# First tap of the scan's convolution made on GpSimd, and two units' first pieces projected a chunk sooner

## The reference

```python
zxbcdt = u @ Wi.T                        # z: 256, xBC: 512, dt: 4 columns
conv = jax.lax.conv_general_dilated(xBC_t, conv_w, (1,), 'VALID', feature_group_count=CONV_DIM, ...)
xBC = jax.nn.silu(jnp.moveaxis(conv, 1, 2) + conv_b)      # 4 taps along time, a filter for each channel
dt = jax.nn.softplus(dt + dt_bias)
def step(h, inp):                        # over the 1024 tokens
    dA = jnp.exp(dt_t * A)
    h = h * dA[..., None, None] + (dt_t[..., None] * x_t)[..., None] * B_t[:, None, None, :]
    y_t = jnp.einsum('bhpn,bn->bhp', h, C_t)
y = (y + D * x) * silu(z)
y = y * rsqrt(mean(y * y) + 1e-05) * norm_w
return y @ Wo.T
```

## Time and profile before

| | |
|---|---|
| median of 3 runs | 825.32 us (821.44 to 828.21) |
| the profiled execution, its own time | 819.01 us |
| its span, first to last instruction | 817.2 us |
| busy in the span: PE, DVE, ACT, POOL | 715.5, 489.4, 542.0, 275.2 us |
| mean granted TensorE clock | 0.955 of full speed |
| the scan's stretch, chunks 0 to 31 | about 471 to 674 us |

### The profile page before, as it was taken

How to read it: one execution, slowest core, us unless ns; L and a number is a source line. 1 busy time by engine, 2 the same in 40 slices (tenths; PEclk the granted TensorE clock), 3 DMA queues, 4 the chain that set the end, 5 groups by cost and what they waited for, 6 DMA issues and landing times. The chain is left out here.

```text
span 817.2 us, 13088 instructions
## 1 busy us (share of the span) xinstructions
PE 715.5 (88%) x4076; PEld 377.9 (46%) x4076; DVE 489.4 (60%) x1424; ACT 542.0 (66%) x934; POOL 275.2 (34%) x296
## 2 busy tenths in 40 slices
PE   4799999979999997988988867798888987999996
PEld 1432222212223223555655545576575775566564
DVE  6878442204766565763466649789697875533453
ACT  5367998888998993653357666885987642434441
POOL 3090003301000342435522445343443380265552
PEclk9899999999999997999999988899998898999999
DMA  4056934521493311112121031121211231222233
GB/s 136 1 203 165 186 86 88 207 76 53 138 317 85 110 37 40 44 34 62 42 80 46 26 109 60 52 65 53 74 60 50 81 84 39 65 61 57 67 99 92
DMA packets 76409, 70.10 MB, mean 86 GB/s; under 512 B 9687, under 2 KB 60233, under 8 KB 76080
## 3 DMA queue, kind: packets, MB, share of 16 engines
q1 hardware_dynamic: 71024, 60.56, 26.6%
q0 software_dynamic: 5024, 8.54, 3.2%
q10 hardware_dynamic: 288, 0.10, 0.0%
HBM read 41.23 MB, written 29.02 MB: 86 GB/s over the span
## 5 line engine op out<-in xcount | busy, mean ns | idle before, releaser
L693 ACT ACTIVATE attn_p<-attn_ps 128x1024 f32<-128x1024 f32 x256 | 241.1, 1083 | 28.5 <-PE attn_ps L686 17.2
L709 PE MATMUL attn_ps<-attn_p,attn_v 128*32 128x512 f32 x1024 | 138.1, 611 | 5.5 <-issue 5.5
L1687 PE MATMUL ps_main<-moe_xsT,moe_w 128*128 128x320 f32 x384 | 127.9, 459 | 8.5 <-DVE moe_hid L1712 3.3
L1697 ACT ACTIVATE moe_act_h<-ps_main 128x320 f32<-128x320 f32 (+1 forms) x128 | 55.2, 434 | 102.5 <-PE ps_main L1687 72.2
L1712 DVE TENSOR_TENSOR moe_hid<-moe_act_h,ps_main 128x320 f32<-128x320 f32 (+1 forms) x128 | 61.9, 485 | 91.1 <-ACT moe_act_h L1697 57.4
L1580 POOL DMA_INDIRECT moe_slots<-rows,moe_scatter_at x64 | 63.4, 991 | 103.0 <-DVE moe_hid L1712 53.8
L1687 PEld LDWEIGHTS ps_main<-moe_xsT,moe_w 128*128 128x128 f32 x384 | 68.8, 195 | 42.5 <-issue 21.8
L686 PE MATMUL attn_ps<-attn_q_rows,attn_k_rows 64*128 64x512 bf16 x448 | 80.6, 388 | 6.4 <-issue 3.1
L1717 PE MATMUL ps_main<-moe_hid,moe_w 128*128 128x320 f32 (+1 forms) x256 | 73.3, 451 | 4.6 <-DVE moe_hid L1712 4.6
L686 PEld LDWEIGHTS attn_ps<-attn_q_rows,attn_k_rows 64*128 64x128 bf16 x448 | 19.1, 93 | 124.0 <-ACT attn_p L693 99.0
L2119 DVE SCALAR_TENSOR_TENSOR mb_act<-mb_padded,mb_taps,mb_act 128x1024 f32<-128x1024 f32 x48 | 65.9, 1382 | 9.0 <-ACT mb_act L2110 8.3
(11 more groups left out here) (268 smaller groups left out, 1304.5 us busy)
## 6 DMA issues: line engine op xcount, KB each, us to landing
mb_cums<-mb_cum_kept SPq DMA_DIRECT2D x32, 256.0 KB, 3.4
moe_slots<-zeros SPq DMA_DIRECT2D x4, 1380.0 KB, 13.4
attn_q_rows<-attn_q_parts SPq DMA_DIRECT2D x36, 128.0 KB
attn_k_rows<-attn_k_parts SPq DMA_DIRECT2D x36, 128.0 KB
moe_w<-in_w SPq DMA_DIRECT2D x3, 1536.0 KB, 11.6
moe_rows<-zeros SPq DMA_DIRECT2D x4, 1024.0 KB, 14.7
moe_back<-moe_rows SPq DMA_DIRECT2D x16, 256.0 KB, 3.8
mb_e_cum<-mb_e_cum_kept SPq DMA_DIRECT2D x56, 64.0 KB, 2.7
```

The costliest lines, as they stand in the source:

```text
L693: self.core.nc.scalar.activation(self.p[:, w % self.PB, :, :].rearrange("p a n -> p (a n)"), self.ps_s[:, w % self.SB, :, :].rearrange("p ...
L709: ins = self.core.nc.tensor.matmul(self.ps_av[32 * i:32 * i + 32, :], self.v[:, b * TPB + kt, (HGROUPS * i + m) // 2, self.window(m)], sel ...
L1687: self.core.nc.tensor.matmul(ps[:, w % 2, 0:CAP], wt[:, e, c * P:(c + 1) * P], self.xsT[:, u % 2, :], start=True, stop=True).then_inc(self ...
L1697: self.core.nc.scalar.activation(self.act_h[into, w % 2, :], self.ps_h1[rows, w % 2, 0:CAP], ACT.Silu).then_inc(self.silu_done, 1)
```

## The change

The first taps of units 1, 2 and 3 (12 instructions of 128x1024 elements) go from ScalarE to GpSimd, as a tensor_scalar (times the tap, times 1.0), with the same waits. GpSimd makes that of piece 0 in chunk i = 0 between to_state and gate, and those of pieces 1, 2 and 3 in chunks 1, 2 and 3 behind decay. Unit 0's stay on ScalarE. `project` and `take` of piece 0 of unit 1 move from chunk 0 to ahead of the loop (on TensorE behind before(0) and ahead of before(1), on ScalarE behind exps(0) and ahead of exps(1)), and those of unit 3 from chunk 16 to the end of chunk 15. Those of unit 2 stay in chunk 8.

```diff
+    def first_tap_beside(self, pool, u, c):
+        src, tap = self.window(u, c, 0)
+        pool.wait_ge(self.proj_read, (u * self.PIECES + c) * 2 + 2)
+        if u >= 2:
+            pool.wait_ge(self.y_read, self.NC * (u - 1))
+        self.core.nc.gpsimd.tensor_scalar(self.act_t[:, u % 2, c, :], src, tap, 1.0, ALU.mult, ALU.mult).then_inc(self.tapped, 1)
@@ tensor
                 mamba.before(pe, 0)
+                mamba.project(pe, 1, 0)
                 for g in range(N):
...
                         for c in mamba.PIECES_AT[i]:
-                            mamba.project(pe, u + 1, c)
+                            if c or u == 1:
+                                mamba.project(pe, u + 1, c)
+                    if u == 1 and i == 7:
+                        mamba.project(pe, u + 2, 0)
@@ gpsimd
                         mamba.to_state(pool, g + 1)
+                    if u < 3 and i == 0:
+                        mamba.first_tap_beside(pool, u + 1, 0)
                     if u < 3:
                         mamba.gate(pool, nc.gpsimd, g)
                     if i < NC - 1:
                         mamba.decay(pool, g + 1)
+                    if u < 3 and i in (1, 2, 3):
+                        mamba.first_tap_beside(pool, u + 1, i)
@@ scalar
                 mamba.exps(act, 0)
+                mamba.take(act, 1, 0)
                 for g in range(N):
...
                         for c in mamba.PIECES_AT[i]:
-                            if c < 4:
+                            if 1 <= c < 4 or (u, c) == (1, 0):
                                 mamba.take(act, u + 1, c)
-                                mamba.first_tap(act, u + 1, c)
...
+                    if u == 1 and i == 7:
+                        mamba.take(act, u + 2, 0)
```

## The result

The changed kernel took 831.72 us, the median of 17 runs (823.65 to 838.64), against 821.16 for the kernel before in as many (816.01 to 828.21). The ratio is 1.0105 [1.0079, 1.0132] (the brackets are its 95% interval): 1% slower, about 8.6 us. The forecast was 834.8, 9.5 us slower than the 825.3 that was then the median of three runs.

A forecast was written before the change was run, and what follows sets the result against it. VectorE's list was taken to bound chunks with taps. Losses of 3.2, 3.75 and 2.5 us in units 0, 1 and 2 make 9.45, say 9.5, on a median of 825.3: 834.8 us, range 829 to 845.

The forecast's parts named there:

- rival 4: Turns fall otherwise, nothing lost in chunks 2 and 3: 831.5 us; low part of the forecast, which has 0.52.
- What bounds the kernel: Chunks with taps last as long as VectorE's list; time taken off ScalarE there shortens nothing.
- The price of a tap: One 128x1024 first tap on GpSimd: 1.04 us, an estimate; the tap as a scalar from SBUF left open.
- Rival 3: The tap on GpSimd is dearer: 839.8 us at 1.54 each, 848 at 2.37; chance 0.2.
- Chunk 1: Each unit: VectorE waits for piece 1's tap behind gate and decay on GpSimd; loss 1.9 us, three times, 5.7.
- Chunk 2: GpSimd's tap holds back VectorE's mb_mt or taps; loss 0.55 us in unit 0, 0.75 in units 1 and 2.
- Chunk 3: Tap comes between combine's adds in unit 0, loss 0.95 us; mb_mt waits in units 1 and 2, 0.15 each.
- Chunk 0 of unit 0: Taps start 3.9 us sooner, but the stall goes to the DMA of exps(2), before mb_mt(2); gain 0.2 us.
- rival 2: Delay partly made up by exps(2)'s rows landing sooner, up to 3.9 us, or unit-end slack; 830 us, chance 0.23.
- Chunk 0 of unit 1: Gate queued behind the tap takes its turn between VectorE's taps, 3.65 us in place of 2.60; net loss 0.95.
- Chunk 0 of unit 2: Early copy delays mb_mt(17); taps start at 587.5 and not 588.12 but meet the gate; gain 0.3 us.
- the turns: GpSimd and VectorE instructions with two SBUF inputs alternate, first asker next; a tap goes between VectorE's work, not beside it.

The follow-up runs named there:

- e8: Kernel before with unit 1's piece 0 projected early, mb_cums of chunk 2 loaded sooner, all 12 taps on GpSimd between to_state and gate; 824.23 us, ratio 1.002.
- e6: Kernel before plus 15 unread 128x1024 multiplications on GpSimd behind decay, chunks 1 to 5 of units 0 to 2; 828.72 us, one run.
- e2: Kernel before with only the 12 first taps moved to GpSimd, nothing projected sooner; 833.47 us, ratio 1.0158.
- e3: Changed kernel with piece 1's tap between to_state and gate in chunk 1; 826.5 us, ratio to before 1.0062.
- e4: Changed kernel with mb_cums of chunk 2 loaded ahead of the fetch of the experts' results; 831.21 us, ratio to before 1.0094.
- c1: Kernel before, unchanged, profiled once more; 822.97 us, one run.
- c2: Changed kernel, unchanged, profiled once more; 828.3 us, one run.
- e7: Kernel before with only unit 1's piece 0 made a chunk sooner and mb_cums of chunk 2 loaded ahead of the fetch, taps on ScalarE; 821.29 us, ratio 0.9989.
- e5: Kernel before with piece 0 of units 1 and 3 made a chunk sooner and mb_cums of chunk 2 loaded ahead of the fetch; 822.15 us, ratio 0.9997.
- e1: Kernel before with only piece 0 of units 1 and 3 projected and copied a chunk sooner, taps on ScalarE; 824.26 us, ratio 1.0013.

## Why the prediction was right, and where it wasn't

Right in sign and size: 9.5 us forecast, 8.6 by the ratio and 8.0 in the scan. The forecast in us, 834.8, stood on a base of three runs that was 4.2 us above the median of the 17. That 831.72 lies on rival 4's 831.5 is this base and chance: chunks 2 and 3 did lose time.

**What bounds the kernel** held. VectorE's list set the chunks with taps: with 13.8 us taken off ScalarE, chunks 1 to 3 of every unit took at least as long as before in e8, but for 0.07 us in one, and in the changed kernel none was shorter by over 0.05.

**The price of a tap** was 1.11 to 1.12 us where it waited for nothing, forecast 1.04. In e6 the same shape with its factors given in the instruction took 1.04. The 0.08 goes with the tap as a scalar from SBUF, or with the row's other source; e6 changes both. Rival 3 is out. The Trainium skill, GPSIMD Engine Reference, section 3.1, would have made it 1.54 by the estimate from its best case; the measurement decides.

**Chunk 1**: 1.9 forecast three times, 5.7 in all; measured 1.90, 1.76 and 1.90. It was shown twice: e2 has it without the early projection, and e3 takes 4.6 of it away by the tap's place alone.

**Chunk 2**: 2.05 forecast, 1.75 measured. The mechanism was as written: the tap starts just ahead of `mb_mt`, and VectorE's busy time in interval 3 grew from 5.40 to 5.91 us, as much as the interval. e6 shows it with a multiplication that nobody needs. The Trainium skill, SBUF — State Buffer, section "SBUF: two separate sides", has the lock behind it; `mb_mt` at 1.47 and not 0.69 beside the tap agrees.

**Chunk 3**: 1.25 forecast, 0.7 measured. Unit 0 lost 0.8 of the 0.95; in units 1 and 2 the 0.15 each were not to be seen (-0.05).

**Chunk 0 of unit 0** was mis-sized: a gain of 0.2 was forecast, 1.5 measured between the pairs' means (16.44 and 14.92; by single profiles 0.4 to 2.6). The step that the stall goes to the DMA of exps(2) held, and e4 shows it: with the DMA sooner 2.0 to 2.5 us more come back. What failed is that I took the instant of the DMA's landing from one execution. There exps(2) began 13.70 us after the start of the scan, and in the second profile of the same kernel, c1, at 11.28:

```profile
488.77 1.28 ACT L2159 ACTIVATE mb_e_seg<-mb_cums,mb_cum_col 128x128 f32<-128x128 f32 x4 [0.59 <-DMA mb_cums<-mb_cum_kept]
```

In the two profiles of after it is 11.79 and 11.28. Between the two with 11.28 the gain is 0.9 us (15.60 and 14.66). The stall before `mb_mt`(2) was 2.81 and 2.31 us and not about 3.5. Part of rival 2 came true here, but it gave 0.7 to 1.3 us and not 3.9.

**Chunk 0 of unit 1**: a loss of 0.95 forecast, 0.1 measured against the mean of two profiles of before that differ by 1.2 (10.65 and 9.47). The mechanism is in the rows: tap, gate behind it at 543.63, VectorE's first instruction at 1.74. The pair took 3.29 us there and not the 3.65 forecast, as decay met only its end. The mean hides the size. The first profile of before had a mean granted clock of 0.65 in interval 7, just ahead, and c1 had 0.87, near the 0.88 of both profiles of after. Against c1 the loss is 0.7 us (9.47 and 10.15). Chunk 0 of unit 2 in e2, with the same order of instructions and a clock of 1.00 as before, gives the same: interval 17 took 8.12 us against 7.40, and the pair

```profile
600.88 3.29 DVE L2126 SCALAR_TENSOR_TENSOR mb_act<-mb_padded,mb_taps,mb_act 128x1024 f32<-128x1024 f32 x2 [2.14 <-POOL mb_act L2117]
```

3.29 us against 2.61. So the term was about 0.7.

**Chunk 0 of unit 2**: a gain of 0.3 forecast, 0.2 measured. The wait went from the tap to `mb_mt`, as worked out:

```profile
596.50 1.37 DVE L2198 TENSOR_TENSOR mb_mt<-mb_e_seg,mb_gm 128x512 f32<-128x512 f32 x1 [1.11 <-ACT mb_e_seg L2173]
...
598.13 0.41 DVE L2281 COPY mb_y_in<-ps_main 128x256 f32<-128x256 f32 x1
```

These are lines of the kernel after; before, `mb_mt` followed its Exp at once at 0.69 us. Its 1.37 here was not in the sum.

**Not in the sum**: about 0.4 us in interval 15, 0.55 in interval 23 and 0.5 in unit 3, 1.5 in all. The second profile of before has interval 15 at 7.42, so that one isn't the taps'; e2, with all of the taps, has 23 at 8.64 and unit 3 at 38.33, nearly as before, so the taps alone don't make these either. In interval 23 the 0.55 us are a wait: `mb_xdt` stands 1.01 us behind TensorE in the profile after and 0.45 in that of before. Why TensorE is later there is open, and so is the rest. They and the misses above nearly cancel: 9.45 less 1.3 (chunk 0 of unit 0), 0.85 (of unit 1), 0.3 (chunks 2), 0.55 (chunks 3) and 0.15 (chunks 1), plus 0.1 and 1.5, is 7.9. These are differences of means. Between c1 and c2, alike in the DMA's landing and in the clock at unit 1's border, the scans differ by 8.9 us, with a gain of 0.9 and a loss of 0.7 in the chunks 0 of units 0 and 1 and only 0.15 left in interval 15. Either way the total was better than its terms, since misses of both signs cancelled, and that is luck.

My account of the turns was right for the places where they fell, and too general: I took 2.05 and 1.25 us as the price of giving GpSimd such work, and e8 shows that elsewhere in the same chunk it costs 0 to 0.5 us each.

## What to carry to other kernels

Work moved to an engine with idle time joins an in-order queue: look at what stands ahead of it there and how long that waits. Here one place in the queue was worth 4.6 of 8 us. On GpSimd look also at which instructions of VectorE it lies beside: next to ones that read PSUM it was free, next to ones with both inputs in SBUF it cost 0.4 to 0.8 us though nobody waited for its result. And when a stall is removed, find the next input due at the same point, here a DMA issued behind four others of its size, before counting the gain. A gain that shows in one unit and not in the whole isn't yet a gain: look at the granted clock at the next border before giving the loss there a cause.

## What the runs showed of the hardware

At the units' borders TensorE idles while the SiLU chain runs, and its granted clock behind that differs between executions. At unit 1's border it stood idle for 0.85 us ahead of L2141 in c1 and for 2.65 in e7. Windows of interval 8, in c1:

```profile
535.37:538.38 3.01, 3.01 (x21) 1.83 (x15) 1.90 (x6) 3.01 (x10) 1.30 (x2) 1.00 0.14 40
```

and in e7:

```profile
530.59:534.60 4.01, 4.01 (x27) 3.60 (x26) 1.98 (x5) 3.07 (x9) 1.34 (x2) 0.74 0.19 63
```

The columns are as in the earlier trace rows; the clock is the third from the end, 1.00 and 0.74 of 2.4 GHz. The same four matmuls of piece 0, at unit 2's start, first in e3 and then in the kernel after, each with the window of just their length:

```profile
586.06 3.76 PE L2083 MATMUL ps_side<-norm_xT,mb_w_xbc 128*128 128x512 f32 x4
```

```profile
586.06:589.82 3.76, 3.76 (x7) 1.59 (x7) 1.44 (x3) 1.33 (x3) 0.72 (x1) 0.50 0.13 42
```

```profile
591.52 1.96 PE L2083 MATMUL ps_side<-norm_xT,mb_w_xbc 128*128 128x512 f32 x4
```

```profile
591.52:593.48 1.96, 1.96 (x8) 0.96 (x8) 0.10 (x1) 1.95 (x3) 0.00 (x0) 1.00 0.34 103
```

A granted clock of 0.50, the 1.2 GHz level, and 3.76 us; 1.00, the 2.4 GHz level, and 1.96 us. Intervals 8 and 9 lay between 9.47 and 12.47 us over all profiles, and this is where the 1.7 to 3.4 us gained in unit 0 by e5 and e7 went. At unit 2's border the profiles fall into two sets. The two of before, the two of after, e2 and e4 have a mean granted clock of 1.00 in intervals 15 and 16 and take 9.2 to 10.2 us in 16 and 17. e1, e3, e5, e6, e7 and e8 have 0.66 to 0.71 in interval 15 and take 11.3 to 12.4. Both sets hold kernels with and without the early projection. The wait ahead alone doesn't decide it: TensorE stood idle for 2.65 us there both in the kernel after, where the clock stayed at 1.00, and in e1, where it was 0.50 within 2 us. Nor does a faster unit 0: e8 had the fastest, 55.04 us, and took 10.15 in intervals 8 and 9, while e6, with 61.25, took 12.47. What decides it these runs don't tell. So one profile can't size a term that has a border in it, while the inner chunks of the table repeat to 0.02 us.
